# The feed-forward of a decoder layer: every expert for every token, or only each token's two experts on rows sorted through DRAM

## The reference

```python
temp = jnp.maximum(temperature, 0.1)
scores = (jnp.einsum('btd,ed->bte', x, router_w) + router_b) / temp
gates = _sinkhorn(scores)                     # three rounds over experts and over a batch's tokens
topk_vals, topk_idx = jax.lax.top_k(gates, 2)
topk_gates = topk_vals / (jnp.sum(topk_vals, axis=-1, keepdims=True) + 1e-08)
g = jax.nn.relu(jnp.einsum('btd,edf->btef', x, wg))
p = jnp.einsum('btd,edf->btef', x, wp)
all_out = jnp.einsum('btef,efd->bted', g * p, wo)
expert_out = jnp.sum(jnp.take_along_axis(all_out, topk_idx[..., None], axis=2) * topk_gates[..., None], axis=2)
return x + expert_out                         # then x + that, and the last layer norm
```

## Time and profile before

| | us |
|---|---|
| median of 3 runs (lowest, highest) | 1088.37 (1087.03, 1089.48) |
| span of the profiled execution | 1083.9 |
| PE busy | 1014.5 (94%) |
| DVE busy | 775.1 (72%) |
| ACT busy | 701.3 (65%) |
| POOL busy | 514.4 (47%) |
| DMA | 14.46 MB, 13 GB/s over the span |

### The profile page before, as it was taken

The page is one execution under the profiler, slowest core; times in us unless marked ns, Lnnn a source line. Parts: engine busy times, 40 slices in busy tenths (PEclk is TensorE's granted clock), DMA queues, the critical chain, the costliest instruction groups (busy, mean ns, idle before and its releaser), DMA issues. The chain is left out here.

```text
span 1083.9 us, 24953 instructions
## 1 busy us (share of the span) xinstructions
PE 1014.5 (94%) x7692; PEld 821.1 (76%) x7692; DVE 775.1 (72%) x2061; ACT 701.3 (65%) x2313; POOL 514.4 (47%) x777
## 2 busy tenths in 40 slices
PE   5999999999999999999999999995399999999996
PEld 3677777777778777777777777773288888888886
DVE  3688888888888888888888888885386445544554
ACT  4787888878888788888888888872832222222221
POOL 4744565455654556545665456630323233323333
PEclk9999999999999999999999999996599999999999
DMA  4000000000000000000000000000300000000000
GB/s 116 9 8 11 8 12 7 7 10 7 12 7 7 10 10 10 7 7 10 11 9 7 7 10 10 5 2 0 117 1 10 1 10 10 10 0 10 10 10 10
DMA packets 22520, 14.46 MB, mean 13 GB/s; under 512 B 3296, under 2 KB 21472, under 8 KB 22240
## 3 DMA queue, kind: packets, MB, share of 16 engines
q1 hardware_dynamic: 22496, 14.15, 4.4%
HBM read 12.05 MB, written 2.10 MB: 13 GB/s over the span
## 5 line engine op out<-in xcount | busy, mean ns | idle before, releaser
L1063 ACT ACTIVATE gs<-ps 128x512 f32<-128x512 f32 x128 | 76.4, 599 | 208.7 <-PE ps L1259 208.7
L409 ACT ACTIVATE prob<-ps,negmax 128x128 f32<-128x128 f32 x512 | 182.1, 420 | 1.2 <-DVE negmax L515 1.2
L417 ACT ACTIVATE xprob<-ps,xmax 128x128 f32<-128x128 f32 x512 | 145.5, 428 | 18.5 <-DVE xmax L515 18.5
L336 POOL TENSOR_TENSOR prob<-prob,recip 128x512 f32<-128x512 f32 x128 | 137.2, 1081 | 35.7 <-DVE recip L520 35.7
L1029 POOL TENSOR_TENSOR acc<-acc,part 128x512 f32<-128x512 f32 x64 | 82.6, 1290 | 143.0 <-DVE part L1192 141.2
L345 POOL TENSOR_TENSOR qk_sin<-qk,sin_sb 128x128 f32<-128x128 f32 x256 | 114.3, 466 | 70.9 <-ACT qk L397 70.5
L409 ACT ACTIVATION_READ_ACCUMULATOR prob<-ps,negmax 128x1 f32 x512 | 133.3, 260 | 0.0
L1267 PEld LDWEIGHTS ps<-fwo_sb,h 128*128 128x128 f32 x1024 | 124.0, 192 | 5.6
L1146 DVE TENSOR_TENSOR h<-ps,gs 128x512 f32<-128x512 f32 x128 | 87.6, 689 | 54.9 <-PE ps L1259 53.8
L1267 PE MATMUL ps<-fwo_sb,h 128*128 128x128 f32 x1024 | 124.4, 275 | 0.0
L360 POOL TENSOR_TENSOR ve<-mv,eps 128x1 f32<-128x1 f32 x64 | 12.1, 189 | 208.3 <-DVE mv L538 208.3
(11 more groups left out here) (163 smaller groups left out, 2396.1 us busy)
## 6 DMA issues: line engine op xcount, KB each, us to landing
xf<-in_x SPq DMA_DIRECT2D x32, 64.0 KB, 1.8
xres<-in_x SPq DMA_DIRECT2D x32, 64.0 KB, 1.7
cx<-in_ctx SPq DMA_DIRECT2D x32, 64.0 KB, 1.8
out_y<-yo SPq DMA_DIRECT2D x8, 256.0 KB, 2.3
fstage<-in_fwg SPq DMA_DIRECT2D x1, 1024.0 KB, 5.2
fstage<-in_fwp SPq DMA_DIRECT2D x1, 1024.0 KB, 7.4
qk<-in_wqkv SPq DMA_DIRECT2D x1, 768.0 KB, 4.6
prob<-in_wqkv SPq DMA_DIRECT2D x1, 768.0 KB, 5.8
```

The source lines that it names most:

```text
L336: nc.gpsimd.tensor_tensor(prob[:, n], prob[:, n], recip[:, n, :, None].broadcast_to([128, 4, S]), ALU.mult).then_inc(normed, 1)
L409: last = nc.scalar.activation(prob[:, n, j, :], bank(name)[:, j * S:(j + 1) * S], ACT.Exp, bias=negmax[:, n, j:j + 1], accum_out=sums[:, n ...
L417: last = nc.scalar.activation(xprob[:, n, g, :], bank(name)[:, g * S:(g + 1) * S], ACT.Exp, bias=xmax[:, n, g:g + 1])
```

## The change

The attention stage keeps its work but for the split of x2, which goes. In its slot 3 SP now also loads the expert weights and fills two DRAM tensors `placed` with zeros. The activation table that holds exponential and logarithm is loaded once at the start.

The feed-forward stage is new. The batches form two groups of 16. For each group the Sinkhorn chain runs on tiles of 128x128, then DVE and two counting matmuls give each (token, expert) pair a row in a list sorted by expert, where each expert's part begins at a multiple of 128 (`place`), and the owner of each 128 rows (`owner`). A group has 2 x 16 + 7 = 39 blocks of 128 rows, 78 in all. Both groups are routed before the first block. POOL writes the rows of x2 to their places with one indirect DMA per batch and choice (`dispatch`, 32 a group). For each block SP loads 128 rows; PE transposes them; ACT and DVE split them; PE multiplies by the owner's gate and value weights (three 128x512 matmuls, the weights moving, at an address from a register that `value_load` fills); ACT and DVE make the hidden rows; PE transposes them back in two halves and multiplies by the output weights; DVE copies the answer and SP stores it in DRAM. When a group's blocks are stored, POOL gathers each token's two answers, for four batches at a time (`gather`, 8 indirect DMAs), and DVE joins and normalises them (`join`, `normalise`). For the first group this stands beside blocks 51 to 76 (`JOINED`, `FINISHED`), for the second behind the last block.

The core of the diff:

```diff
+        fw_hi = keep("fw_hi", [128, 2 * E * FF], F32R)
+        fw_lo = keep("fw_lo", [128, 2 * E * FF], F32R)
+        fwo_sb = keep("fwo_sb", [128, E * FF])
+        tri = keep("tri", [128, 128])
+        ones = keep("ones", [128, 128])
+        zeros = keep("zeros", [128, D])
+        plan = Sparse([16, 16])
+        placed = [nc.dram_tensor(f"placed{g}", [n * 128, D], F32, kind="Internal").ap() for g, n in enumerate(plan.blocks)]
+        cleared = sem("cleared")
...
+                if isinstance(s, int) and s == 3:
+                    pair = fw_lo[:].bitcast(F32).rearrange("p (e a f) -> p e a f", e=E, a=2)
+                    for a_, src in enumerate((fwg, fwp)):
+                        sp.dma_start(pair[:, :, a_, :], src.rearrange("p (e f) -> p e f", e=E)).then_inc(f_loaded, 16)
+                    sp.dma_start(fwo_sb[:].rearrange("p (n d) -> p n d", d=D), fwo.rearrange("(n p) d -> p n d", p=128))\
+                        .then_inc(fo_loaded, 16)
+                    sp.wait_ge(const_ready, 5)
+                    for rows in placed:
+                        n = rows.shape[0] // 128
+                        sp.dma_start(rows.rearrange("(n p) d -> p n d", p=128), zeros[:, None, :].broadcast_to([128, n, D]))\
+                            .then_inc(cleared, 16)
...
+            nc.scalar.preload_act_table_set("natural_log_exp_and_others")
...
-            def split_x2(s, b):
-                drained(dve, s, "c.XT")
-                hi = x2T_hi[:, bass.ds(b * S, S)]
-                nc.vector.tensor_copy(hi, x2T[:]).then_inc(x2_hi_ready, 1)
...
+class Sparse:
+    def __init__(self, groups):
+        self.first = [sum(groups[:g]) for g in range(len(groups))]
+        self.size = list(groups)
+        self.blocks = [2 * n + E - 1 for n in groups]
+        self.block0 = [sum(self.blocks[:g]) for g in range(len(groups))]
+        self.total = sum(self.blocks)
+        self.group_of = [g for g, n in enumerate(self.blocks) for _ in range(n)]
+        self.quads = [(g, self.first[g] + FB * q) for g in range(len(groups)) for q in range(groups[g] // FB)]
...
+        JOINED = {0: 51, 1: 58, 2: 65, 3: 72}
+        FINISHED = {0: 55, 1: 62, 2: 69, 3: 76}
...
+            def load(i):
+                g, p = plan.group_of[i], i % NX
+                if i == plan.block0[g]:
+                    sp.wait_ge(scattered[g], 16 * 2 * plan.size[g])
+                wait(sp, xt_filled, i - NX + 1)
+                at_row = (i - plan.block0[g]) * 128
+                sp.dma_start(xg[p][:], placed[g][at_row:at_row + 128, :]).then_inc(xg_loaded[p], 16)
...
+            def store(i):
+                g = plan.group_of[i]
+                at_row = (i - plan.block0[g]) * 128
+                sp.wait_ge(y_done, i + 1)
+                sp.dma_start(answered[g][at_row:at_row + 128, :], ysb[i % NY][:]).then_inc(y_stored[i % NY], 16)
...
+            for i in range(3):
+                load(i)
+            for i in range(NB):
+                if i >= 2:
+                    store(i - 2)
+                if i + 3 < NB:
+                    load(i + 3)
...
+            def dispatch(g):
+                pool.wait_ge(cleared, 16 * G)
+                pool.wait_ge(rt_dve, dve_after(g, SLOT))
+                for b in range(plan.size[g]):
+                    for k in range(2):
+                        nc.gpsimd.indirect_dma_start(
+                            placed[g], bass.IndirectOffsetOnAxis(place[g][:, k, b:b + 1], 0), x2_all[:, plan.first[g] + b, :], None,
+                            bounds_check=plan.blocks[g] * 128 - 1, oob_is_err=False).then_inc(scattered[g], 16)
+            def gather(q):
+                g, b = plan.quads[q]
+                if b == plan.first[g]:
+                    for p in range(NY):
+                        pool.wait_ge(y_stored[p], 16 * stores_before(p, plan.block0[g] + plan.blocks[g]))
+                wait(pool, acc_step, 3 * (q - 1))
+                for j in range(FB):
+                    for k in range(2):
+                        nc.gpsimd.indirect_dma_start(
+                            yg[q % 2][:, k, j, :], None, answered[g],
+                            bass.IndirectOffsetOnAxis(place[g][:, k, b - plan.first[g] + j:b - plan.first[g] + j + 1], 0),
+                            bounds_check=plan.blocks[g] * 128 - 1, oob_is_err=False).then_inc(gathered[q % 2], 16)
...
+            dispatch(0)
+            dispatch(1)
+            gather(0)
+            for q in range(1, len(plan.quads)):
+                g, b = plan.quads[q]
+                opens = b == plan.first[g]
+                if opens:
+                    rstd(q - 1)
+                gather(q)
+                if not opens:
+                    rstd(q - 1)
+            rstd(len(plan.quads) - 1)
...
+            def split_x(i):
+                act.wait_ge(xt_filled, i + 1)
+                wait(act, up_filled, i - 1)
+                nc.scalar.activation(x_hi[i % 2][:], ps[:, XT, 0:128], ACT.Copy).then_inc(hi_done, 1)
+            def relu(i):
+                act.wait_ge(up_filled, i + 1)
+                wait(act, h_done, i - 1)
+                nc.scalar.activation(gs[i % 2][:], ps[:, UP[i % 2], 0:FF], ACT.Relu).then_inc(relu_done, 1)
+            def hidden_back(i):
+                act.wait_ge(ht_filled, i + 1)
+                wait(act, y_filled, i - 1)
+                nc.scalar.activation(hT[i % 2][:].rearrange("p c s -> p (c s)"), ps[:, HT, 0:FF], ACT.Copy).then_inc(ht_done, 1)
...
+            split_x(0)
+            for i in range(NB + 1):
+                if i + 1 < NB:
+                    split_x(i + 1)
+                if i < NB:
+                    relu(i)
+                if i >= 1:
+                    hidden_back(i - 1)
...
+            def answer(i):
+                dve.wait_ge(y_filled, i + 1)
+                wait(dve, y_stored[i % NY], 16 * stores_before(i % NY, i))
+                nc.vector.tensor_copy(ysb[i % NY][:], ps[:, DOWN, 0:D]).then_inc(y_done, 1)
...
+            def join(q):
+                g, b0 = plan.quads[q]
+                a, y = acc[q % 2], yg[q % 2]
+                dve.wait_ge(gathered[q % 2], 16 * 2 * FB * (quads_before(q % 2, q) + 1))
+                wait(dve, yo_ready, FB * (q - 1))
+                for k in range(2):
+                    for j in range(FB):
+                        own = x2_all[:, b0 + j, :] if k == 0 else a[:, j, :]
+                        last = nc.vector.scalar_tensor_tensor(a[:, j, :], y[:, k, j, :],
+                                                              weight[g][:, k, b0 + j - plan.first[g]:b0 + j - plan.first[g] + 1],
+                                                              own, ALU.mult, ALU.add)
+                    last.then_inc(acc_step, 1)
+                    dve.wait_ge(acc_step, 3 * q + k + 1)
+                nc.vector.tensor_tensor(a[:], a[:], x2_all[:, b0:b0 + FB, :], ALU.add).then_inc(acc_step, 1)
+                dve.wait_ge(acc_step, 3 * q + 3)
+                for j in range(FB):
+                    nc.vector.bn_stats(st3[:, j, :], a[:, j, :]).then_inc(st3_ready, 1)
...
+            def x_transpose(i):
+                p = i % NX
+                pe.wait_ge(xg_loaded[p], 16 * (i // NX + 1))
+                wait(pe, lo_done, i)
+                nc.tensor.transpose(ps[:, XT, 0:128], xg[p][:], ident[:]).then_inc(xt_filled, 1)
+            def expert_up(i, at_col):
+                pe.wait_ge(lo_done, i + 1)
+                wait(pe, h_done, i - 1)
+                dst, p = ps[:, UP[i % 2], :], i % 2
+                hi, lo = fw_hi[:, bass.ds(at_col * 2, 2 * FF)], fw_lo[:, bass.ds(at_col * 2, 2 * FF)]
+                nc.tensor.matmul(dst, x_lo[p][:], hi, start=True, stop=False)
+                nc.tensor.matmul(dst, x_hi[p][:], hi, start=False, stop=False)
+                nc.tensor.matmul(dst, x_hi[p][:], lo, start=False, stop=True).then_inc(up_filled, 1)
+            def hidden_back(i):
+                pe.wait_ge(h_done, i + 1)
+                wait(pe, ht_done, i)
+                for c in range(FF // 128):
+                    last = nc.tensor.transpose(ps[:, HT, c * 128:(c + 1) * 128], h[i % 2][:, c * 128:(c + 1) * 128], ident[:])
+                last.then_inc(ht_filled, 1)
+            def expert_down(i, at_col):
+                pe.wait_ge(ht_done, i + 1)
+                wait(pe, y_done, i)
+                for c in range(FF // 128):
+                    last = nc.tensor.matmul(ps[:, DOWN, 0:D], hT[i % 2][:, c, :], fwo_sb[:, bass.ds(at_col + c * 128, 128)],
+                                            start=(c == 0), stop=(c == FF // 128 - 1))
+                last.then_inc(y_filled, 1)
+            for k in range(STAGES):
+                route(0, k)
+            for k in range(STAGES):
+                route(1, k)
+            pe.wait_ge(f_lo, 4)
             pe.wait_ge(fo_loaded, 16)
+            pe.wait_ge(rt_dve, dve_after(0, TABLE))
+            owners = {}
+            x_transpose(0)
+            for i in range(NB + 2):
```

(32 more changed lines are left out.)

605 lines of the change are left out of this document (316 added, 289 removed).

## The result

The changed kernel takes **1162.3 us** (median of 4 runs, 1159.9 to 1166.2) against 1088.9 before: ratio 1.069, 95% interval 1.066 to 1.072. Slower by 6.9%, where 1079 and at most 1130 had been forecast. The profiled execution took 1161.4 us, its span 1159.7.

What follows compares the result with a forecast made beforehand. PE was taken to bound both stages of the kernel before. 758.4 of attention + 28 + 39 + 198 + 50.5 gave a 1074 us span, carried over to 1079 us against 1088.4; range 1035 to 1130.

Steps and rivals of the forecast that it cites:

- Term 3: Feed-forward, the 78 blocks: 198 us, from 2.38 us a block, 3 for filling and draining, 10 for four joins.
- term 2: Before the first block, POOL's 32 scatters for the first group: 39 us at 1.15 us each; the second group's cost nothing.
- term 4: Tail behind the last block: second group's gathers, join, normalise and store, 50.5 us; the first group's gathers are covered.
- The loop of 2.38 us per block: In the blocks, the store-then-load round through DRAM takes 4.75 us for two blocks and sets their pace.
- Term 1: Start of the feed-forward, routing the first group (Sinkhorn iterations, then placing): 28 us, bounds 24 and 36.
- Attention at nothing: Attention stage: fewer DVE operations and 8.1 MB more through SP's ring change nothing; it ends at 758.4 as before.
- wrong if attention ends anywhere but at 758: Sign for the attention stage: an end at any time other than 758 us would show the forecast wrong.
- the 4.5 us: Whole kernel: profiled span lies 4.5 us under the runs' median, so a span of 1074 became 1079 us.
- The clock: Rival, in the blocks: PE's clock falls to 1.2 GHz, 2.75 us a block, 29 us more, 1108 us; chance 0.20.
- Dear indirect DMAs: Rival, scatters and tail gathers: 1.9 us per indirect DMA, 48 us more, 1127 us, break-even 1.3; chance 0.14.
- DVE and POOL locking each other out: Rival, in four joins and the tail beside POOL's gathers: perhaps 5 us, inside the range; no chance of its own.

Runs made afterwards that it cites:

- x4_spaced: Changed kernel with each of the second group's 32 scatters waiting for one more block of the first group; 1121.3 us.
- x5_paced: On top of x4_spaced, each of the first group's 32 gathers waits for one more second-group block, joins stand 8 blocks apart; 1096.8 us.
- x11_before_table: Kernel before the change, with only the one table for exp and ln loaded at the start; 1083.9 us, ratio 0.997.
- x1_both_first: Changed kernel with the first block's load waiting for both groups' scatters, so no block runs beside a scatter; 1160.1 us.
- x7_probe: Changed kernel plus useless work beside the second group's scatters: DVE copies without waits, ACT copies with waits, PE transposes in a loop; 1185.9 us, one execution.
- x8_probe: As x7_probe with roles changed: DVE a loop with semaphore waits, ACT copies and PE transposes written out without waits; 1205.5 us, one execution.
- x14_half_rows: Changed kernel with the second group's 32 scatters moving 64 of each batch's 128 rows; 1160.5 us.
- x15_end: On top of x5_paced: six row buffers, loads five blocks ahead, joins in three pieces, last quad's reciprocal root on ACT instead of POOL; 1041.3 us, ratio 0.958.

## Why the prediction was wrong

- **Term 3, the blocks, is the step that failed**, and in it one sentence of term 2: that the second group's 32 scatters run beside the first 39 blocks and "cost nothing unless one takes over 2.4 us", with its twin in term 4 for the gathers. They take 1.27 us, so by that rule they were free. In fact the blocks nearly stood still beside them: 41.0 us went with pacing the scatters (x4_spaced), 24.5 more with pacing the gathers and moving the joins apart (x5_paced), 65.5 of the 70.7 us. I had asked only whether POOL would be in time, and not what a dense row on POOL does to the others.
- **The loop of 2.38 us per block** was right. Undisturbed blocks came every 2.33 to 2.48 us, PE's waits ended at the load, and taking the loop away gave 1.68. PE's own work in a block was put too low, 1.3 us against 1.68: a down product is two matmuls in the program and four in the trace, and I had counted two, and where the kind of matmul changes the next starts 0.20 to 0.33 us later instead of 0.117 or 0.235 (930.13, 930.33, 930.66). So PE was 74% busy and not 55%, which changed nothing in the sum.
- **Term 1** 29.7 against 28: right, and 2.1 of the 29.7 are attention's later end in this execution. **Term 2** 42.2 against 39: an indirect DMA costs 1.27 of POOL, not 1.15, for 0.97 us of work and a gap of 0.30. The Trainium skill's figure that I had named, about 1 us to the first byte (DMA: Bandwidth & Descriptors, Latency and other measured facts), which it puts down to GpSimd's work, is near the 0.97 that GpSimd is busy; the gap comes on top. No run here was read for the first byte itself.
- **Term 4** 60.7 against 50.5: the gathers with two rstd between them took 45.1 instead of 39.3 (32 times 1.31 is 41.9, and the two rstd take 1.5 each), and 4.7 us come from POOL's DRAIN, which no term had.
- **Attention at nothing** was right, to 1 us of PE's time. The 8 MB through SP's ring delayed single loads (an xres landed 9.1 us after its issue, the median is 1.8), but no wait of PE ends at one: from 22 to 58 us PE did 253 matmuls beside that traffic and 251 in x11_before_table, which has none. My sign "wrong if attention ends anywhere but at 758" was too sharp, since its end scatters by 4 us.
- **The sum.** I carried the 4.5 us between the profiled span and the median over to the changed kernel. A run's own time and span lie 1.7 us apart there (1161.44 and 1159.7) and about 2 in the kernel before (1087.77 and 1085.7), so most of the 4.5 was one fast execution, and the forecast should have read 1076. In term 3 the loop's items add up to 4.7 us and not 4.75, and a join's to 2.8 and not 2.5. None of this matters beside the 70.7 us.
- **The rivals.** The clock did read 0.53 from 840 to 880, but behind idle engines, not before them: in the even stretch it is 0.96, and with PE 74% busy it did not stay down. Dear indirect DMAs: 1.27 and 1.31 us are at their break-even of 1.3, and they alone would have cost 9 us. DVE and POOL locking each other out: the probe's copies last as long in the standstill as after it, and ACT and PE were held as well, so it was not that. None of the rivals had a row of cheap operations on POOL that holds up engines which do not wait for it, and their range ended at 1130.
- What the change removes, 325 us of PE-bound stage, is truly gone. With the row of DMAs paced, the loads ahead, the joins cut and POOL's last work moved to ACT, the same idea is 4.2% faster than the kernel before, instead of 6.9% slower.

## What to carry to other kernels

That operations overlap on the timeline, and that no one waits for them, does not make them free. Pace indirect DMAs from POOL by the work that runs beside them (here one per block, or 1.7 us apart by time alone), rather than issuing them in a row; where nothing ran beside them (x1_both_first) a row cost nothing further. If every engine slows at once and its idle time ends at "issue", look for what one of them is doing in that time rather than for a missing wait.

## What the runs showed of the hardware

- While POOL issued indirect DMAs 1.27 us apart, DVE, ACT and PE each started one instruction per 1.40 us, whatever it was: 0.17 us or 0.37 us long, with or without a wait, in a loop or written out. It began 19 to 27 us behind the first DMA and ended 9 us behind the last, as a backlog would: from the first scatter to the end it lasted 89.8 to 90.5 us in x7_probe, x8_probe, x14_half_rows and the changed kernel, and 64 times 1.40 is 89.6. That it is a queue is inferred from these times.
- It depends on the distance (80 matmuls of blocks in 20 us at 1.67 us, 49 at 1.46, 18 at 1.30), not on the rows (64 or 128), and 32 plain DMAs of the same size from the same queue, 0.54 us apart, do not cause it.
- What is shared stays open. The Trainium skill, in NOTIFIC — the notification-queue block (7.1 Overflow: three behaviours, one of which stalls the engine), tells of a block that collects the engines' records and can hold its producers back when a queue is full. No run here shows whether it is that: each run's span and clock are read from such records, so it also stays open whether the slow-down, and with it these times, would be the same in an execution without them.
- POOL's closing DRAIN took 8.98 us in every kernel with indirect DMAs (9.00 in x15_end, where POOL's last work ends 5 us earlier), 1.13 us in the two without.
